# FFN blocks in pairs in the odd slots, and a ring of four activations, in a fused SSD and mixture-of-experts kernel

## The reference, cut to what matters

```python
x = x + attn(layernorm(x))     # rmsnorm, projection, causal conv, silu, scan over chunks, gate, rmsnorm, projection
x = x + ffn(layernorm(x))
# ffn: two shared experts and four routed ones, hidden width 512, output width 128
sh = relu(einsum('bsd,ndf->bsnf', x, sw1) + sb1)
shared = (einsum('bsnf,nfo->bsno', sh, sw2) + sb2).sum(axis=2) / 2
rh = relu(einsum('bsd,edf->bsef', x, rw1) + rb1)
eo = einsum('bsef,efo->bseo', rh, rw2) + rb2
routed = (take(eo, top2_index) * top2_weight).sum(axis=2)   # weights: softmax of x @ gate_w + gate_b
# ffn(x) = shared + routed
```

## Time and profile before

| what | value |
|---|---|
| median of three runs | 759.35 us (758.93 to 760.9) |
| the profiled execution's own time | 760.49 us |
| its span, first to last instruction | 758.4 us |
| mean granted TensorE clock | 0.946 of full |
| PE busy | 656.0 us, 86% |
| DVE busy | 477.1 us, 63% |
| ACT busy | 359.9 us, 47% |
| POOL busy | 176.7 us, 23% |

### The profile page before, as it was taken

The page is one execution under the profiler, slowest core; times in us unless marked ns, Lnnn a source line. Parts: engine busy times, 40 slices in busy tenths (PEclk is TensorE's granted clock), DMA queues, the critical chain, the costliest instruction groups (busy, mean ns, idle before and its releaser), DMA issues.

```text
span 758.4 us, 11829 instructions
## 1 busy us (share of the span) xinstructions
PE 656.0 (86%) x3890; PEld 514.7 (68%) x3890; DVE 477.1 (63%) x1148; ACT 359.9 (47%) x837; POOL 176.7 (23%) x249
## 2 busy tenths in 40 slices
PE   4477869989889988989889988999989988988896
PEld 3355857677767766777767766777767766776664
DVE  6654266566766587467767587467767587465544
ACT  3624136634564346644655346544655346542252
POOL 7146110323013210323014110323014110232002
PEclk9879579999999999999999999999999999999799
DMA  7000000000000000000000000000000000000000
GB/s 230 8 15 2 1 0 1 15 1 1 0 29 1 1 1 1 29 1 1 0 28 0 0 0 8 20 0 0 0 28 0 0 1 15 1 1 0 15 1 14
DMA packets 12345, 8.89 MB, mean 12 GB/s; under 512 B 1259, under 2 KB 10902, under 8 KB 12310
## 3 DMA queue, kind: packets, MB, share of 16 engines
q1 hardware_dynamic: 12310, 8.44, 3.6%
HBM read 6.34 MB, written 2.10 MB: 11 GB/s over the span
## 4 chain that ended last, share of the span: by engine, by line
PE 49%; DVE 24%; issue 6%; ACT 5%; POOL 0%; DVEq 0%; POOLq 0%; ACTq 0%
PE bank L485 7%; PE bank L360 6%; PE bank L362 5%; PE bank L361 5%; PE bank L464 4%; PE bank L562 4%; PE bank L563 3%; PE bank L564 3%; DVE act_l L1105 3%; PE bank L478 2%; PE bank L473 2%; ACT decay L781 2%; DVE cv L933 2%; PE bank L506 1%; PE bank L441 1%
## 5 line engine op out<-in xcount | busy, mean ns | idle before, releaser
L757 ACT ACTIVATE act_h<-bank 128x512 fp32r<-128x512 f32 x192 | 116.8, 609 | 205.2 <-PE bank L362 203.2
L1105 DVE SCALAR_TENSOR_TENSOR act_l<-bank,act_h 128x512 fp32r<-128x512 f32 x192 | 131.2, 687 | 117.3 <-ACT act_h L757 115.3
L360 PE MATMUL bank<-fTl,w1h 128*128 128x512 f32 x192 | 92.2, 480 | 22.1 <-DVE fTl L1060 11.2
L1299 POOL TENSOR_TENSOR late<-late 128x512 f32<-128x512 f32 x32 | 41.4, 1293 | 259.7 <-DVE late L1113 259.7
L781 ACT ACTIVATE decay<-bank,lneg 128x128 f32<-128x128 f32 x256 | 71.2, 382 | 35.4 <-PE bank L441 35.4
L562 PE MATMUL bank<-act_l,w2h 128*128 128x512 f32 x192 | 80.1, 417 | 3.7 <-DVE act_l L1105 2.2
L563 PE MATMUL bank<-act_h,w2l 128*128 128x512 f32 x192 | 78.0, 406 | 0.0
L362 PE MATMUL bank<-fTh,w1h 128*128 128x512 f32 x192 | 77.9, 406 | 0.0
L564 PE MATMUL bank<-act_h,w2h 128*128 128x512 f32 x192 | 77.6, 404 | 0.0
L361 PE MATMUL bank<-fTh,w1l 128*128 128x512 f32 x192 | 77.3, 402 | 0.0
L360 PEld LDWEIGHTS bank<-fTl,w1h 128*128 128x128 f32 x192 | 36.8, 191 | 44.5 <-DVE act_l L1105 32.6
(11 more groups left out here) (193 smaller groups left out, 1258.3 us busy)
## 6 DMA issues: line engine op xcount, KB each, us to landing
x_in<-L_attn_hidden_dram SPq DMA_DIRECT2D x8, 256.0 KB, 2.8
out_dram<-late SPq DMA_DIRECT2D x8, 256.0 KB, 2.8
late<-L_ffn_sw_dram SPq DMA_DIRECT2D x2, 512.0 KB, 6.3
late<-L_ffn_rw_dram SPq DMA_DIRECT2D x1, 1024.0 KB, 6.7
CT<-L_attn_w_in_proj_dram SPq DMA_DIRECT2D x1, 772.0 KB, 4.6
b_dt<-L_attn_b_dt_dram SPq DMA_DIRECT2D x1, 128.0 KB, 3.3
w_out_raw<-L_attn_w_out_proj_dram SPq DMA_DIRECT2D x1, 128.0 KB, 3.5
rows<-L_ffn_sb_dram SPq DMA_DIRECT2D x1, 4.0 KB
```

Of the source, the lines that this page charges most:

```text
L360: mm(dst, stat_h, mov_l, start=True, stop=False)
L757: nc.scalar.activation(act_h[:, b % RING, :], HID[b % 2][:], ACT.Relu).then_inc(act_h_ready, 1)
L1105: v_.scalar_tensor_tensor(act_l[:, r, :], HID[b % 2][:], 0.0, f(act_h[:, r, :]), ALU.max, ALU.subtract)\
L1299: g.tensor_tensor(acc, acc, term, ALU.add).then_inc(acc_ready, 1)
```

## The change

A new function gives the blocks of a slot as a list: in an odd slot those of the slot before and of its own, in an even slot none. `first`, `second`, `relu` and `act_low` are called over this list. So in an odd slot PE runs its scan part, two `first`, and the two `second` of the pair that was begun two slots before; an even slot holds scan work alone. `RING` grows from three to four buffers. The two `second` after the loop stay as they are, and so do the slots of all other steps, among them `shared_out` and `routed_out`, which read `FOUT`.

```diff
-RING = 3
+RING = 4
...
+        def pair_at(i, prev, older):
+
+            return [q for q in (block_at(i - 1, prev, older), block_at(i, prev, older)) if q] if i % 2 else []
+
...
-                    if new := block_at(i, prev, older):
+                    for new in pair_at(i, prev, older):
                         first(*new)
                     if prev is not None and i == LATE - 1:
                         f_transposes(s, prev)
-                    if old := block_at(i - LAG, prev, older):
+                    for old in pair_at(i - LAG, prev, older):
                         second(*old)
...
-                    if new := block_at(i, prev, older):
+                    for new in pair_at(i, prev, older):
                         relu(*new)
...
-                    if new := block_at(i, prev, older):
+                    for new in pair_at(i, prev, older):
                         act_low(*new)
```

## The result

The changed kernel takes 840.74 us (median of four runs, 838.09 to 844.42), the kernel before 759.67 beside it: a ratio of 1.107, interval 1.102 to 1.111. It is 81 us slower. The profiled execution has a span of 838.8 us.

The account below looks back on a forecast made before the run. PE's matmul queue bounds the kernel; 26 us of stalls in seven bodies, 1 in the two without a scan and 21 of lost clock make 48 on 759.35, 807, rounded to 808 us; range 782 to 842.

Parts of the forecast that it names:

- this term alone: PE stalls: 14.1 us a body for 9.2, 26 us over seven bodies, plus 1 in the two without a scan.
- the first rival: Whole kernel: the new stalls come but the granted clock stays as it is; 786 us, chance 0.22.
- the clock: Sparse places in seven bodies: the granted clock falls to half, 2.5 falls a body, 21 us more than now.
- The sure place: Start of y_product of chunk 2 to end of segments of chunk 3: one clock fall counted in each body.
- the five uncertain ones: Slots 10 and 11, 14 and 15, 16 and 17, 18 and 19, and slot 3: three in ten for a fall each.
- the long place: From y_product of chunk 2 to the end of segments of chunk 3: 7 us with no large matmul.
- Stalls alone: Whole kernel: the stalls come, 26 + 1 us, with the clock unchanged; 786 us, chance 0.22.
- A fall at every sparse place: All six sparse places of a body: the clock falls at each, 64 us in all; 850 us, chance 0.12.
- Faster: DVE and ACT chains run ahead, the three largest new stalls vanish, 2.9 us less a body; 740 us, chance 0.05.
- no change: Whole kernel: odd-slot stalls that go are worth what the even slots cost; 759 us, chance 0.03.
- the three large stalls: New stalls at segments of chunk 3 (2.92 us), transposes of chunk 1 (2.27) and segments of chunk 1 (1.39).
- The edges: Change between a block's matmuls and small products: ten pairs save about 0.12 us each, 1.2 us a body.

Follow-up runs that it names:

- e1: The changed kernel with thrown-away 128x512 matmuls put into its PE stalls, the waits themselves left in place: 788.46 us, ratio 1.037 to the kernel before.
- e8: The changed kernel with thrown-away matmuls only around the first half of the segments of chunk 3: 822.38 us, ratio 1.081 to the kernel before.
- e10: The kernel of e6 with thrown-away matmuls in its remaining PE stalls: 774.5 us over six runs, ratio 1.008 from the three quicker ones.
- e11: As e10, but the four thrown-away matmuls before the weight rows go to the other hidden bank: 750.62 us, ratio 0.988 to the kernel before.
- e6: The kernel before with single blocks moved: none in slots 4 and 5, one each from slot 6, two in slots 17 and 20; 755.02 us, ratio 0.993.

## Why the prediction was right, and where its size was off

**Direction and mechanism.** The cover went from the even slots, and the waits came back where the layout put them. Counted from the starts as in the prediction: block 22 2.62 (2.44 forecast), the gate 0.66 (0.73), `lparts` 1.5 (1.60), weight rows 1.3 (1.19), block 4's `first` 0.6 (0.86), `lcs` 0.3 (0.30), `segments` of chunk 1 1.4 (1.39), transposes of chunk 1 2.3 (2.27), `segments` of chunk 3 2.9 (2.92). The stalls that were to vanish (`segments` of chunk 2, the transposes of chunk 0, the last `second`) did. In time, e1 shows this term alone: 28 us for the 27 forecast, 788.5 for the first rival's 786. The forecast's own sum is 807; 808 is a slip of rounding that changes nothing. That 840.7 still lies in the stated range is close to luck: its upper end, 842, held by little more than 1 us.

**The step that was mis-sized is the clock.** I counted one sure fall and three in ten at each of five other places, 2.5 a body and 21 us more in all. Five a body came, and they cost 52 us, as taking them away shows. What failed in that step is the chance. The sure place fell in all seven bodies. Of the five uncertain ones, those behind `lcs` and at `segments` of chunk 1 fell in all seven too, the one behind `gram` and `y_product` of chunk 1 in five, slot 3's in three, and the one at the transposes of chunk 1, with a stall of 2.3 us, in two. The clock also fell behind the gate in slot 5 in four bodies (one of them as before), a place that I had not counted. The price of a fall, 1.7 us, held on the average: 35 falls at 1.7 less the 8.6 us of today would be 51 us for the 52 measured, though the long place alone cost 2.6 a body (e8) and the others less. Of the 33 us by which 808 was short, this term is 31.

**The rivals.** "Stalls alone" is e1, and it was out by just the clock. "A fall at every sparse place" (850) was nearer the result than my own forecast (808). By the rule of the Trainium skill ("TensorE: Matmul & The Clock Gate", "A second HAM failure mode: psum-queue depth-cycling"), which I had put behind that rival, falls at all six places were to be expected; the trace agrees in the main, with five falls a body and a mean of 0.873, but not at every place, as counted above. The argument against it, that most sparse places of the kernel before pass at full clock, was read from places that had a block of six large matmuls on either side; the change takes exactly these away. That this is why they passed is argued; e1, which puts large matmuls back, fits it. "Faster" and "no change" are out: the three large stalls came in full. The two bodies without a scan take 65.4 us from the start of the first to the end, for 65.9 before, where the forecast had +1 (-2 to +4).

**The edges.** A pair should save 0.12 us of edges. The traces show it at `gram` of chunk 0, where a block before and a pair after stand between the same two small steps:

```profile
393.05 0.50 PE L360 MATMUL bank<-fTl,w1h 128*128 128x512 f32 x1
...
394.55 1.00 PE L478 MATMUL bank<-xw,btok 128*128 128x64 f32 x8
```

```profile
433.65 0.50 PE L364 MATMUL bank<-fTl,w1h 128*128 128x512 f32 x1
...
436.53 1.00 PE L482 MATMUL bank<-xw,btok 128*128 128x64 f32 x8
```

A block took 1.50 us from start to start, two of them 3.00; the pair takes 2.88. That is 0.12 here; the other places were not measured.

## What to carry to other kernels

A filler block between two dependent steps is worth what it covers at that place, so before blocks are merged for fewer switches, lay the other engines' answers out slot by slot: here that gave each stall to 0.3 us. Then ask what the matmul engine's clock does in the sparse stretches that result; pricing them as if each fell came nearer here than three in ten, and this second cost was nearly twice the first. And where a wait can't be covered with useful work, large matmuls that are thrown away keep the clock, as long as what they write to is free without a wait (e10 beside e11).

## What the runs showed of the hardware that I had not expected

A matmul engine that runs useless matmuls in its waits (up to 2.9 us each) got through the work behind them sooner than one that rests: 317 thrown-away matmuls (4207 instructions of PE for 3890) brought 52 us. A place need not have a wait for the clock to fall behind it: `gram` and `y_product` of chunk 1 run one after the other with PE busy throughout, 4.00 of 4.00 us in the stretch from 448.00, and yet the clock goes to 0.85 and 0.72 there; in e1, which fills waits alone, it still fell behind this place in three bodies. Before that fall the engine had run nothing but small matmuls since 446.15, without a pause. And the falls differ from run to run: e6 spread over 751 to 759 us with a clock from 0.958 to 0.942, e11, which differs by the fill, over 749.5 to 752.1.
